# Two self attentions of a fused transformer kernel: values mixed with a row per query, scaled out of the bank, then turned

## The reference

```python
# first layer: 16 query heads, 2 key/value heads of 32 channels, biases, causal
Q, K, V = (x @ Wq + bq), (x @ Wk + bk), (x @ Wv + bv)      # split into heads
scores = where(causal, -inf, Q K^T / sqrt(32))
out = softmax(scores) V                                     # back to 512 channels
return out @ Wo + bo
# second layer: 16 heads, q and k normalised per head and rotated, no bias
q = rotate(rmsnorm(q)); k = rotate(rmsnorm(k))
return (softmax(mask(q k^T / sqrt(32))) v) @ w_out
# first feed-forward block
h = fwht(x * SU_ug) / 64                                    # fwht: Walsh-Hadamard transform
z = silu(h @ W_gate.T * g) * (h @ W_up.T * u)
y = (fwht(z * SU_dp) / 64) @ W_down.T * s
```

## Time and profile before

| | us |
|---|---|
| median of 3 runs | 2293.49 |
| lowest, highest | 2290.13, 2294.36 |
| profiled execution | 2287.49 |
| its span | 2285.7 |

### The profile page before, as it was taken

How to read it: one execution, slowest core, us unless ns; L and a number is a source line. 1 busy time by engine, 2 the same in 40 slices (tenths; PEclk the granted TensorE clock), 3 DMA queues, 4 the chain that set the end, 5 groups by cost and what they waited for, 6 DMA issues and landing times.

```text
span 2285.7 us, 27993 instructions
## 1 busy us (share of the span) xinstructions
PE 2118.2 (93%) x8810; PEld 1430.8 (63%) x8810; DVE 1169.6 (51%) x2688; ACT 773.6 (34%) x1962; POOL 995.4 (44%) x953
## 2 busy tenths in 40 slices
PE   7998999999888999999997999998994999999995
PEld 5865766577557864566664666656773555555552
DVE  4226777645634112355554777758765343444443
ACT  2124433323231110133334433434422444445451
POOL 1027465312237210177767475447511444455552
PEclk8998999999999999999999999998985999999998
DMA  3231001110021100011122010110033799988886
GB/s 115 83 110 54 19 26 35 31 61 1 19 92 37 50 33 0 0 51 51 39 72 88 18 28 21 67 63 1 1 129 135 244 300 303 265 216 210 221 210 163
DMA packets 84545, 209.21 MB, mean 92 GB/s; under 512 B 13857, under 2 KB 39969, under 8 KB 76929
## 3 DMA queue, kind: packets, MB, share of 16 engines
q1 hardware_dynamic: 61680, 153.54, 19.7%
q0 software_dynamic: 21280, 51.38, 11.0%
q10 hardware_dynamic: 1440, 2.49, 0.3%
HBM read 257.95 MB, written 34.36 MB: 128 GB/s over the span
## 4 chain that ended last, share of the span: by engine, by line
PE 52%; DVE 9%; ACT 4%; POOL 3%; issue 2%; DMA 1%; SPq 0%; POOLq 0%; ACTq 0%; DVEq 0%
PE banks L98 32%; PE banks L854 4%; PE banks L2204 3%; PE banks L2205 3%; DVE L1x_prob L541 2%; ACT L1x_prob L489 2%; PE banks L2179 2%; DVE L1x_small L528 1%; DVE L1x_pT_lo L509 1%; PE banks L448 1%; PE banks L1299 1%; POOL L1a_part_s L1541 1%; POOL L1a_tiny L1515 1%; PE banks L2169 1%; PE banks L1689 1%
## 5 line engine op out<-in xcount | busy, mean ns | idle before, releaser
L98 PE MATMUL banks<-L1f_w,L1f_xT 128*128 x760 | 264.1, 491 | 2.1 <-ACT L1f_xT L2272 1.1
L2453 POOL DMA_INDIRECT moe_sums<-L1f_y,L1f_row x95 | 150.7, 1586 | 220.5 <-DVE L1f_is_who L2325 153.9
L159 POOL TENSOR_TENSOR rstd<-rstd,power 128x1 f32<-128x1 f32 x48 | 30.0, 624 | 368.6 <-DVE rstd L153 368.6
L98 PEld LDWEIGHTS banks<-L1f_w,L1f_xT 128*128 128x128 f32 x760 | 137.8, 191 | 81.6 <-issue 6.2
L2461 POOL DMA_INDIRECT L1f_xg<-moe_rows,L1f_row x95 | 94.2, 991 | 73.9 <-DVE L1f_row L2320 47.7
L448 PE MATMUL banks<-L0x_wn,L0x_qT 128*128 128x512 f32 x256 | 115.1, 593 | 0.8 <-DVE x L518 0.8
L448 PE MATMUL banks<-L1x_wn,L1x_qT 128*128 128x512 f32 x256 | 115.1, 593 | 0.8 <-DVE x L518 0.8
L2292 DVE SCALAR_TENSOR_TENSOR L1f_z<-banks,L1f_share,L1f_sg 128x192 f32<-128x192 f32 x95 | 39.7, 418 | 146.4 <-ACT L1f_sg L2227 146.4
L489 ACT ACTIVATE L0x_prob<-banks,L0x_small 128x256 f32<-128x256 f32 x128 | 59.0, 472 | 159.9 <-DVE L0x_small L531 159.9
L489 ACT ACTIVATE L1x_prob<-banks,L1x_small 128x256 f32<-128x256 f32 x128 | 59.0, 472 | 158.1 <-DVE L1x_small L531 158.1
L98 PE MATMUL banks<-L0f_down,L0f_z 128*128 128x512 f32 x256 | 111.1, 592 | 1.5 <-DVE L0f_z L1787 1.5
(11 more groups left out here) (389 smaller groups left out, 5353.9 us busy)
## 6 DMA issues: line engine op xcount, KB each, us to landing
L1f_w<-in_experts SPq DMA_DIRECT2D x95, 1280.0 KB
L1f_laid<-moe_counts SPq DMA_DIRECT2D x59, 512.0 KB, 5.4
w<-in_L1x_heads SPq DMA_DIRECT2D x16, 704.0 KB, 4.1
w<-in_L0x_heads SPq DMA_DIRECT2D x16, 608.0 KB, 3.7
w<-in_wug SPq DMA_DIRECT2D x8, 1024.0 KB, 4.8
L0x_craw<-in_ctx SPq DMA_DIRECT2D x96, 64.0 KB, 2.0
L1x_craw<-in_ctx SPq DMA_DIRECT2D x96, 64.0 KB, 2.0
w<-in_L0x_out SPq DMA_DIRECT2D x4, 1280.0 KB, 6.4
```

The costliest lines, as they stand in the source:

```text
L98: ins = pe.e.matmul(out, w, m, start=first and n == 0, stop=last and n == len(pairs) - 1)
L2453: pool.e.indirect_dma_start(self.sums[j % 2][:, :], bass.IndirectOffsetOnAxis(ap=self.row[:, j:j + 1], axis=0), self.y[j % self.NY][:], No ...
```

## The change

Values are now mixed with a 128x32 piece of pTb as weights and 128 columns of vbd streamed, so a row of the bank is a query. DVE multiplies it by the inverse sum on the way out of the bank into `on`; PE turns it back into the same bank (`turn_values`, four transposes); ACT copies that with the permutation to oTb (`keep_values`). POOL's multiplication of the weights is gone, and `turn_weights` waits for the exponential alone. ACT's value spreading is put behind these copies. The tail of each attention is written out in another order, and L0f's folds no longer wait for `begin`: they use banks 3 and 4, wait for the last copy of turned weights, and ACT copies them ahead of the row work.

```diff
     def turn_weights(self, pe, i):
-        pe.wait_ge(self.weighed, i + 1)
+        pe.wait_ge(self.exped, i + 1)
...
     def mix(self, pe, i):
+        for b in range(BPT):
+            for t in range(AT):
+                ins = pe.e.matmul(bank[b * S:(b + 1) * S, t * P:(t + 1) * P], pt[:, t, b * S:(b + 1) * S],
+                                  vb[:, b, t // self.tpg, :], start=True, stop=True)
+        ins.then_inc(self.mixed.sem, 1)
+    def turn_values(self, pe, i):
+        bank = self.mix_bank("values", i)
+        pe.wait_ge(self.weighed, i + 1)
         for t in range(AT):
-            for b in range(BPT):
-                at = t * P + b * S
-                ins = pe.e.matmul(bank[:, at:at + S], vb[:, b, t // self.tpg, :], pt[:, t, b * S:(b + 1) * S], ...)
+            ins = pe.e.transpose(bank[:, t * P:(t + 1) * P], self.on[:, t * P:(t + 1) * P], self.sh.ident[:])
+        ins.then_inc(self.o_turned.sem, 1)
...
     # ACT, step i: exponential of i-3, keys of i-2, then
+            if 0 <= i - 5 < NT - 3:
+                self.keep_values(act, i - 5)
+            if 0 <= i - 4 < NT - 1:
+                self.keep_weights(act, i - 4)
+            ... (tail: keep_values(i - 5) of steps 10 to 12, keep_weights(7) in step 10)
+            if 0 <= i - 2 < NT:
+                self.spread_values(act, i - 2)
+    def keep_values(self, act, i):
+        act.wait_ge(self.o_turned, i + 1)
+        act.wait_ge(self.projected, i - 1)
+        act.e.copy(self.oTb[i % 2][:].rearrange("p t (s b) -> p t b s", s=S), ...)
...
     def keep_mixed(self, dve, i):
         dve.wait_ge(self.mixed, i + 1)
-        dve.wait_ge(self.projected, i - 1)
-        dve.e.tensor_copy(self.oTb[i % 2][:]...)
+        dve.wait_ge(self.summed, 2 * i + 2)
+        dve.wait_ge(self.o_turned, i)
+        dve.e.tensor_tensor(self.heads(self.on[:]), self.heads(self.mix_bank("values", i)), self.of_heads(self.tiny[:, i, 6, :]), ALU.mult)
...
     # POOL, step i
-                pool.wait_ge(self.summed, 2 * s + 2)
-                pool.e.tensor_tensor(pr[:], pr[:], self.of_heads(self.tiny[:, s, 6, :]), ALU.mult)
...
     # HadamardFfn
     def tensor(self, pe):
         self.turn_rows(pe, NT - 2)
+        self.fold_down(pe, 0)
         self.transform_rows(pe, NT - 2)
-        self.begin(pe)
-        self.fold_down(pe, 0)
         self.turn_rows(pe, NT - 1)
...
+        self.begin(pe)
         self.widen_and_down(pe)
     def fold_down(self, pe, q):
+        self.begin_early(pe)
+        for signal, n in self.left_turning:
+            pe.wait_ge(signal, n)
...
-            pe.e.matmul(self.sh.psum(4 + n % 2), ...)
+            pe.e.matmul(self.sh.psum(3 + n % 2), ...)
     def scalar(self, act):
-        self.rows_hi(act, NT - 3)
-        self.keep_rows(act, NT - 2)
-        self.rows_hi(act, NT - 2)
-        self.begin(act)
         for q in range(FC // 4):
             ... four copies of folds (act.e.copy(self.down[:, n, :], ...))
-            if q == 1: self.keep_rows(act, NT - 1)
-            elif q == 2: self.rows_hi(act, NT - 1)
+            if q < 3: self.rows_hi(act, NT - 3 + q)
+            if q < 2: self.keep_rows(act, NT - 2 + q)
+        self.begin(act)
```

More of the change, by code:

```diff
@@ L1214, in tensor @@
     def tensor(self, pe):
-        for i in range(NT + 5):
+        for i in range(NT + 2):
             if i < NT:
@@ L1227, in tensor @@
                 self.spread(pe, i - 2)
+            if 0 <= i - 5 < NT:
+                self.turn_values(pe, i - 5)
             if 0 <= i - 4 < NT:
                 self.turn_weights(pe, i - 4)
-            if self.after:
-                self.after.turn_early(pe, i)
+            self.after.turn_early(pe, i)
             if 0 <= i - 5 < NT:
                 self.project_out(pe, i - 5)
-            if self.after:
-                self.after.ask_early(pe, i)
+            self.after.ask_early(pe, i)
+            self.after.transform_early(pe, i)
+        last = NT + 2
+        self.score(pe, NT - 1)
+        self.mix(pe, NT - 3)
+        self.turn_weights(pe, NT - 2)
+        self.after.turn_early(pe, last)
+        self.mix(pe, NT - 2)
+        self.turn_values(pe, NT - 3)
+        self.turn_weights(pe, NT - 1)
+        self.after.ask_early(pe, last)
+        self.project_out(pe, NT - 3)
+        self.after.transform_early(pe, last)
+        self.after.turn_early(pe, last + 1)
+        self.mix(pe, NT - 1)
+        self.turn_values(pe, NT - 2)
+        self.after.ask_early(pe, last + 1)
+        self.project_out(pe, NT - 2)
+        self.after.transform_early(pe, last + 1)
+        self.turn_values(pe, NT - 1)
+        self.after.turn_early(pe, last + 2)
+        self.after.ask_early(pe, last + 2)
+        self.project_out(pe, NT - 1)
+        self.after.transform_early(pe, last + 2)
     def turn_input(self, pe, i):
@@ L1623, in rows_early @@
     def rows_early(self, dve, i):
+        for t in self.EARLY.get(i - 1, ()):
+            self.scale_rows(dve, t)
         for t in self.EARLY.get(i, ()):
             self.normalise(dve, t)
-        for t in self.EARLY.get(i - 1, ()):
-            self.scale_rows(dve, t)
         for t in self.EARLY.get(i - 2, ()):
@@ L1688, in fold_down @@
             pe.wait_ge(self.down_kept, n - 1)
-            pe.e.matmul(self.sh.psum(4 + n % 2), self.had[:, 1, :], w.ap[:, a * D:(a + 1) * D], start=True,
+            pe.e.matmul(self.sh.psum(3 + n % 2), self.had[:, 1, :], w.ap[:, a * D:(a + 1) * D], start=True,
                         stop=True).then_inc(self.down_mixed.sem, 1)
@@ L1730, in scalar @@
                 act.wait_ge(self.down_mixed, n + 1)
[L1731 to L1735, removed]
+                act.e.copy(self.down[:, n, :], self.sh.psum(3 + n % 2)).then_inc(self.down_kept.sem, 1)
+            if q < 3:
+                self.rows_hi(act, NT - 3 + q)
+            if q < 2:
+                self.keep_rows(act, NT - 2 + q)
+        self.begin(act)
         self.split_up_hi(act, 0)
@@ L2082, in ask_early, with transform_early @@
             self.ask(pe, t)
+    def transform_early(self, pe, i):
+        pass
     def keep_early(self, act, i):
@@ L2480, in build_kernel @@
         first.after = stage(SelfAttention, "L0a", KVH, False, first.mixed_all)
-        first.after.after = stage(HadamardFfn, "L0f", first.after.projected_all)
+        first.after.after = stage(HadamardFfn, "L0f", first.after.projected_all, first.after.turned_all)
         second = first.after.after.after = stage(RotatedQueries, "L1x", first.after.after.widened)
```

86 lines of the change are left out of this document (52 added, 34 removed).

## The result

The changed kernel takes 2280.56 us in the median of five runs (2278.22 to 2282.28), the kernel before 2292.61 (2290.13 to 2294.36): ratio 0.9949, 95% interval 0.9934 to 0.9963, 12.0 us less. The forecast was 2275.5, range 2264 to 2288. The profiled execution took 2280.83 us.

The account below looks back on a forecast made before the run. PE, busy 93% of the span, was taken as the bound. Terms -2.4, 0, -0.6, -2, -11.8 and -3.0 sum to -19.8; with 1.7 kept back, -18.1 gives 2275.5 us, own range 2268 to 2282, with rivals 2264 to 2288.

Parts of the forecast that it names:

- Prices: In 16 tiles, a mix loses 1.20 us and turning values adds 0.49: PE's own work changes by -11.4 us.
- A step with all parts: One attention step walked from the mix: projection starts at 5.1 to 5.6 us in L0a, 5.5 to 6.0 in L1a.
- the slow copy: ACT's permuting copy of turned values at the high end, 1.09 us; the sum's gain is then 3 us less.
- L0a's loop, -2.4: L0a's steps 5 to 9: five projection starts add up to 25.5 to 27.9 us, before 29.0; middle -2.4.
- L1a's loop, 0: L1a's steps 5 to 9: five projection starts add up to 32.6 to 35.1 us, before 33.8; middle 0.
- The clock, -2, with 1.7 kept back: Loop projections regain 2 us as falls inside the old mix go; 1.7 us reserved for one new stretch at 1.2 GHz.
- The slow rival: Rival 4: the new wait ahead of projections lowers the clock; at ten of 16 tiles +8, 2301 us; 7%.
- POOL, -0.6: L1a's steps 3 and 4: POOL's dropped multiplication, about 1.05 us a tile, gives -0.6 us.
- L0a's tail and L0f, -11.8: From L0a's last-tile first scores to the first large matmul: 64.8 us shrinks to 53.0, a gain of 11.8.
- rivals 2 and 3: Folds don't fill the gaps, 2284 us, 10%; the new mix is no faster, 2289.5 us, 8%.
- L1a's tail, -3.0: L1a's last scores to last projection's end, before 36.0 us: middle -3.2, less 0.2 for DVE's routing, so -3.0.
- The base: The change of -18.1 us was put on the median, 6.0 us above the profiled execution of 2287.49: 2275.5 us.

Follow-up runs that it names:

- mix_alone: The new mix, scaling, turned values and ACT's copy, with loops, both tails and L0f's folds ordered as in the kernel before; 2286.83 us, ratio 0.9973.
- L1a_old_tail: The changed kernel, but L1a's last three tiles are worked in the order of before; 2277.60 us, ratio 0.9941.
- logits_alone: The changed kernel, but in L1a's tail the router's logits stand behind each projection; 2276.56 us, ratio 0.9921.
- order_alone: The new order of both tails and the folds, with the old mix and POOL's scaling of the weights; 2288.70 us, ratio 0.9979.

## Why the prediction was right, step by step

- **Prices.** The mix (2.39 us), the turning of values (four transposes, about 0.5 us to the next start) and the scaling (0.69) came as forecast. ACT's copy, taken as 0.83 between 0.59 and 1.09, is 1.06: the mis-sized term. The row with the pattern decided, not the row with the engine. The Trainium skill (SBUF — State Buffer, "Door 1: The DMA port swizzle") has the rule that each access to a new line of 16 bytes pays, and this trace agrees: 1.06 against 0.59.
- **A step with all parts.** Counted from the scores, the forecast for the slow copy is 8.0 us (L0a) and 8.4 (L1a) to the projection; measured 8.18 and 8.20. In L0a this is near by luck, since two misses cancel. Scores and mix overlap by 0.52 us, which was not in the walk. And the walk let ACT copy q as soon as it is turned, 3.06 us after the start of the mix; it left out the exponential, which the shorter mix no longer hides, and the copy came at 3.74. Against the old 7.78 each plain step loses 0.4.
- **L0a's loop, -2.4.** This failed: 79.2 and 77.6 us. The step that failed is the path to the projection. Counted from the mix, the five starts of the projection were forecast at 25.5 to 27.9 us together, and measured 33.0 (6.31 three times, 7.03, 7.05). The exponential is late most of all in steps 8 and 9, 3.9 us after the start of the mix, and PE waits for the copy of q there as well:

```profile
568.59 0.66 PE L1315 MATMUL banks<-ident,L0a_pr 128*128 128x128 f32 x4 [1.01 <-ACT L0a_qTb L1409]
```

The overlap of scores and mix gave 2.6 us of this back. The clock is the other part: I compared steps that held low-clock time before, and did not give the new ones any. In all five profiled executions in which this loop is as in the changed kernel, the projections of steps 5 and 8 are slow, 5.4 us and 5.1 or 6.7 us: both of the changed kernel, `mix_alone`, `L1a_old_tail` and `logits_alone`. Against the 80.4 that the old mix took in two of its three profiled executions it is a small gain, against the profile I had, a loss.
- **L1a's loop, 0.** This failed too, by 3.2. Step 8 has it. DVE's late mask holds the scaling, as I said, and the projection starts 12.05 us after the start of the mix (1647.41 to 1659.46; forecast 10.6 to 11.1). What I missed is that PE stands 5.65 us and then works at 1.2 GHz, 6.69 us for the projection:

```profile
1656.55 1.12 PE L1335 MATMUL banks<-ident,L1a_on 128*128 128x128 f32 x4 [5.65 <-DVE L1a_on L1573]
1659.46 6.69 PE L98 MATMUL banks<-w,L1a_oTb 128*128 128x512 f32 x8 [0.94 <-ACT L1a_oTb L1403]
```

```profile
1656.00:1660.00 4.00, 2.51 (x9) 2.07 (x10) 3.69 (x12) 3.90 (x7) 0.00 (x0) 0.50 0.74 177
```

- **The clock, -2, with 1.7 kept back.** The direction was half right. The fall inside the mix of L1a's step 7 did not come back (its projection takes 3.67 in place of 4.87; but the second execution of before has 3.60 there too), and falls came behind the waits instead. The mean granted clock of the loops is about as before: in L0a 0.94 and 0.96 against 0.95 and 0.87, in L1a 0.94 twice against 0.92 and 0.98. The slow rival had the right place, and where it was tested, in L0a's loop, the right mechanism; only four projections paid, not ten.
- **POOL, -0.6.** Measured -0.6, and the loss of the multiplication is what `order_alone` and `mix_alone` tell apart.
- **L0a's tail and L0f, -11.8.** Right, 53.6 us (forecast 53.0, slow copy 53.7). This term carries nearly all of the gain; rivals 2 and 3 fell with it and with the mix.
- **L1a's tail, -3.0.** Half of it came. The walk had the logits' waits, but no low clock behind the first (5.38 in place of 3.67 us), and did not ask what the old order with the new mix would take: 5.1 us less.
- **The base.** I put the difference on the median and counted before's profiled execution as typical in its parts. By the prediction's own lower end (slow copy, no gain of the clock in the loops: -13) the medians' -12 is met. The middle, -18.1, was 6 us too far: the two loops came out 6.6 us worse than forecast and L1a's tail 1.5, and a range of 24 us took that in.

## What to carry to other kernels

A shorter operation in front of a longer chain gives its saving to the wait: follow the chain through every engine's queue, with the operations that the longer one used to hide (here the exponential ahead of the copy of q), and place the copy that PE waits for ahead of copies that are needed only a step later. Put a permutation where it is written for free, here in PE's write to the bank, and not in a copy on the path. Profile the kernel before twice when a few us matter, since the clock's falls can differ by 6 us in a single stretch.

## What the runs showed of the hardware

- PE wrote transposed columns to a bank at every fourth word at no cost (285 ns either way); ACT, writing them to SBUF in that order, took 1.06 us in place of 0.59.
- 32 matmuls with 32 columns of weights and 128 streamed took 2.39 us, with 128 and 32 they took 3.59. Two such groups of the first kind, scores and mix, overlapped at their border and took 4.26 us together.
- The granted clock fell to 0.50 in three surroundings: inside the old mix with PE busy throughout, in the projection behind a wait of 1.3 us that follows transposes, and around one of 5.65 us. With eleven transposes in the wait, or two matmuls, all projections of L0a's loop took 3.6 to 3.7 us. Why steps 6 and 7 with the same wait kept the full clock was not settled.
